# Graph layers on one core: the local numbers of the scores stage in bf16, its attribute transpose one step earlier

## The chip, the cores and the metric

The kernel runs on one core of one Trainium2 chip. The time is the device time of one execution in microseconds. Three runs of the kernel before gave 5438.61, 5443.80 and 5426.68 us, median 5438.61.

## What is computed

Four graph layers follow each other over 3125 nodes of 128 features and 100000 edges, each with a residual and a layer norm. The change lies in the second one, attention over edges. Cut to what matters:

```
q = (x @ Wq + bq).reshape(n, H, C)          # 4 heads of 32
k = (x @ Wk + bk).reshape(n, H, C)
v = (x @ Wv + bv).reshape(n, H, C)
e = (edge_attr @ We).reshape(-1, H, C)      # 32 attributes of each edge
kj = k[src] + e
vj = v[src] + e
alpha = jnp.einsum('ehc,ehc->eh', q[dst], kj) / np.sqrt(C)
```

A softmax of alpha over the edges of each destination node and a weighted sum of vj follow.

## The kernel before, in words

Edges are sorted by destination and cut into tiles of 128. A *pair* is a tile together with a block of 128 nodes to which some of its edges go; there are up to 806 pairs. For each edge of a pair the *local number* is its destination's number less the first node of the block: 0 to 127 means that the edge belongs to the block, anything else that it does not. `index_stage` (L443 on) makes these numbers on VectorE (L558), stores them in DRAM as `loc` (L482) and transposes them for later stages. For the stair "dst", which is the stored one, there are two outputs, `local` and `source`.

`scores` (L1535 on) takes four pairs a step, 202 steps in all, six steps a round (WAYS = 6), with six buffers q = 0 to 5 for most tiles. 33 rounds run in hardware loops on TensorE and VectorE; GpSimd, SyncE and ScalarE have all steps written out. In a step:

- SyncE loads the attribute rows of four pairs (L1600) after the transpose of the same buffer one round before, and the row of 512 local numbers into one partition, `locr` (L1603), after that buffer's spread.
- GpSimd gathers the keys and values of 128 sources, four times (L1592). It waits for `added`, which VectorE's L1644 signals when the buffer is free again.
- TensorE makes, in this order: the transpose of the attribute rows (L1691), eight records of node products (four float32 products of a one-hot tile with `q`, two passes each, L1695), the attribute product (L1699, two passes), and the *spread*, a product of a row of ones with `locr` that copies the 512 numbers to all 128 partitions of PSUM (L1682), for the step two further on.
- ScalarE copies the transposed attributes to SBUF (L1611) and issues the store of k+e and v+e (L1616).
- VectorE makes the one-hot tile by comparing the spread numbers with the partition's number (L1637, "heat"), adds the attribute product to keys and values (L1644), multiplies by q (L1648) and sums over a head (L1651).

`attr_t` and the PSUM tiles have two buffers, which is why most waits of TensorE name the step two before (`before_last`). VectorE's order in a round (L1655 on) is heat 0, heat 1, then heat 2, score 0, heat 3, score 1, heat 4, score 2, heat 5, score 3, score 4, score 5. `softmax_maxima` (L1717 on) reads `loc` back from DRAM and compares it with 0 and 128 (L1821, L1822).

## Time and profile before

| | |
|---|---|
| profiled execution, device time | 5436.53 us |
| its span | 5434.8 us |
| median of the three runs | 5438.61 us |
| mean granted TensorE clock over the span | 0.694 |
| busy: TensorE, VectorE, ScalarE, GpSimd | 3062.4, 2231.2, 614.3, 3413.0 us |
| scores stage | about 1074 to 2380 us |

Busy times are sums over stages that have different limits, so the share of the whole span says little about one stage. In rows of groups and of the timeline, a name such as `sc_kve<-sc_kv,ps` reads "written from". "Idle before" is the time for which that engine had nothing just before the instruction, and the name behind the arrow is what ended the idle time by the profile's reading of semaphores. Starts of TensorE's records are measured; their ends are modelled.

### The profile page before, as it was taken

Reading aid. Unit: us, or ns where it says so; the run is one execution under the profiler, and the core shown is the slowest. Engines: PE = TensorE matmul, PEld = TensorE weight load, DVE = VectorE, ACT = ScalarE, POOL = GpSimd, SP = SyncE. Lnnn points to the kernel's source line nnn. Section 1 sums busy time; section 2 is a strip of 40 time slices with the busy share of each in tenths; the row PEclk is TensorE's granted clock in tenths of the full one; section 3 lists DMA queues with packets and bytes.
Section 4 is the critical chain, followed back from the end, with each engine's and each line's share of the span. In section 5 each row is a group of like instructions: output and inputs, shape, how many; then the busy total and the mean of one; then the engine's idle time right before and its main releaser. Section 6 shows DMA issues by size and latency. Waiting matters only on the chain. (4 is left out here: it accounts for less than half of the span.)

```text
span 5434.8 us, 50013 instructions
## 1 busy us (share of the span) xinstructions
PE 3062.4 (56%) x13750; PEld 2237.6 (41%) x13751; DVE 2231.2 (41%) x2709; ACT 614.3 (11%) x1076; POOL 3413.0 (63%) x3213
## 2 busy tenths in 40 slices
PE   3899989567777777744918633343333333333333
PEld 1788879233333333324917422232222323232223
DVE  7999985445555454568901331111111111101112
ACT  0455540000000000004701000000000000000000
POOL 2888868466556555657770356666666666666664
PEclk7999999666666666657958766665665656555555
DMA  5566667144444444425825332222222111111111
GB/s 177 157 181 192 177 198 230 37 131 138 132 133 139 132 135 130 139 87 159 259 62 195 136 100 70 69 64 60 60 59 60 48 46 46 45 46 46 46 46 46
DMA packets 498663, 599.91 MB, mean 110 GB/s; under 512 B 190115, under 2 KB 367441, under 8 KB 496248
## 3 DMA queue, kind: packets, MB, share of 16 engines
q0 software_dynamic: 117856, 246.12, 16.5%
q1 hardware_dynamic: 337751, 229.77, 14.8%
q10 hardware_dynamic: 42944, 122.68, 6.0%
q8 instruction: 51, 0.84, 0.1%
q14 instruction: 61, 0.49, 0.0%
HBM read 406.69 MB, written 204.36 MB: 112 GB/s over the span
## 5 line engine op out<-in xcount | busy, mean ns | idle before, releaser
L720 POOL DMA_INDIRECT rec_by_src<-rec,pos x782 | 1123.3, 1436 | 524.6 <-issue 238.9
L1132 PE MATMUL ps<-g_got,g_hot 128*128 x3224 | 687.5, 367 | 1225.8 <-issue 797.4
L1132 PEld LDWEIGHTS ps<-g_got,g_hot 128*128 128x128 f32 x3224 | 605.7, 272 | 1320.2 <-issue 1318.9
L1592 POOL DMA_INDIRECT sc_kv<-kv,d_src x806 | 761.8, 945 | 533.9 <-DVE sc_kve L1644 260.2
L1032 POOL DMA_INDIRECT g_got<-y_forward,d_msg x782 | 739.3, 945 | 381.8 <-issue 230.1
L1032 POOL DMA_INDIRECT g_got<-y_back,s_msg x782 | 737.8, 943 | 381.2 <-issue 233.5
L805 PE MATMUL ps<-ln_low,ln_hot 128*125 128x256 f32 x2848 | 620.3, 381 | 20.3 <-DVE ln_low L782 16.1
L805 PEld LDWEIGHTS ps<-ln_low,ln_hot 128*125 128x125 f32 x2848 | 535.6, 188 | 104.8 <-issue 24.4
L1043 DVE TENSOR_TENSOR g_hot<-ps,src_loc 128x1024 f32<-128x1024 f32 x101 | 120.6, 1221 | 992.5 <-remote 450.4
L1699 PE MATMUL ps<-w_e,sc_attrT 128*128 128x512 f32 x404 | 320.0, 887 | 246.0 <-ACT sc_attrT L1611 216.3
L1051 DVE TENSOR_TENSOR g_y<-ps,ms_b 128x384 f32<-128x384 f32 x75 | 41.8, 558 | 808.8 <-remote 474.2
L1695 PE MATMUL ps<-q,sc_hotT 128*128 x1616 | 308.5, 352 | 108.0 <-DVE sc_hotT L1637 92.0
L1644 DVE TENSOR_TENSOR sc_kve<-sc_kv,ps 128x1024 f32<-128x1024 f32 x202 | 244.9, 1212 | 239.2 <-DMA win_rows<-rec_by_dst,win_tilei 163.3
L1695 PEld LDWEIGHTS ps<-q,sc_hotT 128*128 128x128 f32 x1616 | 283.2, 262 | 130.2 <-issue 130.2
L1682 PE MATMUL ps<-sc_locr,ones 1*128 1x512 f32 x404 | 312.8, 864 | 10.4 <-issue 10.4
L1637 DVE TENSOR_SCALAR sc_hotT<-ps,part 128x512 f32<-128x512 f32 x202 | 148.0, 747 | 379.5 <-PE ps L1682 196.3
L1145 PE MATMUL ps<-ms_w,ms_xT 128*128 128x384 f32 x150 | 105.9, 800 | 250.0 <-DVE g_y L1051 166.0
L777 DVE TENSOR_TENSOR ln_low<-col,win_lo 128x1024 f32<-128x1024 f32 x178 | 219.7, 1234 | 4.9 <-PE ps L805 2.6
L782 DVE TENSOR_TENSOR ln_low<-ln_low,win_w 128x1024 f32<-128x1024 f32 x178 | 216.1, 1214 | 0.0
L779 DVE TENSOR_TENSOR ln_hot<-col,win_key 128x1000 f32<-128x1000 f32 x178 | 213.8, 1201 | 0.0
L2030 ACT ACTIVATE n_root<-n_var 128x25 f32<-128x25 f32 x1 | 0.2, 225 | 1812.2 <-DVE n_var L2019 1812.2
L828 ACT ACTIVATE ln_out<-ps 125x1024 f32<-125x1024 f32 x160 | 163.7, 1023 | 311.3 <-PE ps L805 294.5
(323 smaller groups left out, 3283.7 us busy)
## 6 DMA issues: line engine op xcount, KB each, us to landing
linked<-ln_out SPq DMA_DIRECT2D x320, 224.0 KB
ve<-sc_kve ACTq DMA_DIRECT2D x202, 256.0 KB
wv_ve<-ve SPq DMA_DIRECT2D x101, 512.0 KB
l_links<-linked SPq DMA_DIRECT2D x25, 800.0 KB
l_links<-linked ACTq DMA_DIRECT2D x25, 800.0 KB
f_links<-linked SPq DMA_DIRECT2D x25, 800.0 KB
f_links<-linked ACTq DMA_DIRECT2D x25, 800.0 KB
attr_pairs<-ln_feats POOLq DMA_DIRECT2D x7, 2048.0 KB
```

The lines of the kernel that those rows point to most:

```text
L720: pool.indirect_dma_start(out=dram["rec_by_src"], out_offset=bass.IndirectOffsetOnAxis(ap=S["pos"][:, c:c + 1], axis=0), in_=S["rec"][:, c ...
L777: dve.tensor_tensor(low[:, q, :, 0:P], S["col"][:, :].unsqueeze(1).to_broadcast([P, GROUP, P]), S["win_lo"][:, cols].unsqueeze(2).to_broad ...
L779: dve.tensor_tensor(hot[:, q], S["col"][:, 0:KEYS].unsqueeze(1).to_broadcast([P, GROUP, KEYS]), S["win_key"][:, cols].unsqueeze(2).to_broa ...
L782: dve.tensor_tensor(low[:, q, :, P:2 * P], low[:, q, :, 0:P], S["win_w"][:, cols].unsqueeze(2).to_broadcast([P, GROUP, P]), ALU.mult).then ...
L805: last = pe.matmul(ps[0:KEYS, bass.ds(slots[j], 2 * P)], hot[:, q, j, :], low[:, q, j, :], start=False, stop=True, skip_group_check=True)
L1032: pool.indirect_dma_start(out=got[:, (c % SLOTS) * D:(c % SLOTS + 1) * D], out_offset=None, in_=table, in_offset=bass.IndirectOffsetOnAxis ...
L1132: last = pe.matmul(ps[:, bass.ds(columns[j], width)], hot[:, q, j, :], got[:, bass.ds(slots[j], width)], start=False, stop=True, skip_grou ...
L1592: pool.indirect_dma_start(out=kv[:, q, j, :], out_offset=None, in_=dram["kv"], in_offset=bass.IndirectOffsetOnAxis(ap=S["d_src"][:, c:c + ...
L1644: dve.tensor_tensor(kve[:, q].rearrange("p a (k d) -> p k a d", d=D), kv[:, q].rearrange("p k (a d) -> p k a d", a=2), feat(q).rearrange(" ...
L1682: pe.matmul(spread_loc(q), S["ones"][0:1, :], locr[0:1, q, :], start=True, stop=True).then_inc(spread[q], 1)
L1695: pe.matmul(qe(q)[:, j * D:(j + 1) * D], hot_t[:, q, j * P:(j + 1) * P], S["q"][:, bass.ds(cols[j], D)], start=True, stop=True)
L1699: pe.matmul(feat(q), attr_t[:, q % 2, :], S["w_e"][:, :], start=True, stop=True).then_inc(product[q], 1)
```

## The change

The numbers are kept as bf16: a new tile `short` in the index stage is copied from the float32 numbers, and the store takes it; the DRAM array `loc`, the tile `locr` and the tile `mx_loc` become bf16. In `scores` a bf16 row of ones replaces the float32 one, so the spread is a product of two bf16 operands. A wait on `saved` in the index stage is taken out. The transpose of the attribute rows moves out of `step` into `turn_row`, and is issued for the next step behind the attribute product of this one, in front of the spread.

```
+        self.short = m.sb(name + "_short", [P, self.cols], BF16) if stored else None
...
-                                 wide[:, n % 2, 0:s.cols].rearrange("p (b e) -> p b e", e=P)).then_inc(saved, 16)
+                                 s.short[:, :].rearrange("p (b e) -> p b e", e=P)).then_inc(saved, 16)
...
-                        if s.stored and n - 2 == sum(len(t.outputs) for t in stairs[:k]):
-                            dve.wait_ge(saved, 32)
...
                         link(dve.tensor_copy(s.nodes[:, :].rearrange("p (b e) -> p b e", e=P), f[:, :, :, node_field]))
+                        link(dve.tensor_copy(s.short[:, :], wide[:, n % 2, 0:s.cols]))
...
-        locr = m.sb("sc_locr", [1, WAYS, STEP * P])
+        locr = m.sb("sc_locr", [1, WAYS, STEP * P], BF16)
+        ones = m.sb("sc_ones", [1, P], BF16)
...
+            dve.memset(ones[:, :], 1.0).then_inc(cleared, 1)
             dve.memset(S["alpha"][:, :, :], 0.0).then_inc(cleared, 1)
-            dve.wait_ge(cleared, 1)
+            dve.wait_ge(cleared, 2)
...
-                pe.matmul(spread_loc(q), S["ones"][0:1, :], locr[0:1, q, :], start=True, stop=True).then_inc(spread[q], 1)
+                pe.matmul(spread_loc(q), ones[:, :], locr[0:1, q, :], start=True, stop=True).then_inc(spread[q], 1)
+
+            def turn_row(i, q):
+                pe.wait_ge(featured[q], (i + 1) * 16)
+                before_last(pe, kept, q, i)
+                pe.transpose(turn(q), attr[:, q, :], S["ident"][:, :]).then_inc(turned[q], 1)
...
-                pe.wait_ge(featured[q], (i + 1) * 16)
-                before_last(pe, kept, q, i)
-                pe.transpose(turn(q), attr[:, q, :], S["ident"][:, :]).then_inc(turned[q], 1)
...
+            pe.wait_ge(cleared, 1)
             for q in range(2):
                 spread_row(0, q)
+            turn_row(0, 0)
             with pe.Fori(0, WHOLE) as i:
                 for q in range(WAYS):
                     step(i, q)
-                    if q + 2 < WAYS:
-                        spread_row(i, q + 2)
-                    else:
-                        spread_row(i + 1, q + 2 - WAYS)
+                    turn_row(i + (q + 1) // WAYS, (q + 1) % WAYS)
+                    spread_row(i + (q + 2) // WAYS, (q + 2) % WAYS)
...
-        loc = m.sb("mx_loc", [P, L])
+        loc = m.sb("mx_loc", [P, L], BF16)
...
-        "linked": scratch("linked", [2, WINDOWS, KEYS, P]), "loc": scratch("loc", [PAIR_COLS, P]),
+        "linked": scratch("linked", [2, WINDOWS, KEYS, P]), "loc": scratch("loc", [PAIR_COLS, P], BF16),
```

## Rows read from the trace of the kernel before

**Rows 1.** A stretch, scores stage: length; PE, PEld, DVE, ACT, POOL busy (count); clock

```profile
1500.00:1750.00 250.00, 182.12 (x501) 86.58 (x500) 124.86 (x156) 10.53 (x38) 149.79 (x159) 0.65 0.47 135
```

**Rows 2.** Groups of the scores stage: count, busy us, mean ns, idle before, releasers

```profile
L1592 POOL DMA_INDIRECT sc_kv<-kv,d_src x806 | 761.8, 945 | 533.9 <-DVE sc_kve L1644 260.2 <-issue 249.9 <-DVEq L1632 23.9
L1699 PE MATMUL ps<-w_e,sc_attrT 128*128 128x512 f32 x404 | 320.0, 887 | 246.0 <-ACT sc_attrT L1611 216.3 <-issue 29.6
L1682 PE MATMUL ps<-sc_locr,ones 1*128 1x512 f32 x404 | 312.8, 864 | 10.4 <-issue 10.4
...
L1644 DVE TENSOR_TENSOR sc_kve<-sc_kv,ps 128x1024 f32<-128x1024 f32 x202 | 244.9, 1212 | 239.2 <-DMA win_rows<-rec_by_dst,win_tilei 163.3 <-DMA dst_rows<-rec_by_dst,pair_tiles 63.1 <-issue 7.8
...
L1611 ACT ACTIVATE sc_attrT<-ps 128x128 f32<-128x128 f32 x202 | 56.0, 277 | 1263.9 <-remote 548.8 <-PE ps L1691 427.4 <-issue 280.2
```

**Rows 3.** Waits of the scores stage: us in total, times, longest us

```profile
POOL sc_kv L1592 <- DVE sc_kve L1644: 260.2, 79, 7.9
...
DVE sc_hotT L1637 <- PE ps L1682: 196.3, 67, 5.4
```

**Rows 4.** Timeline of one round: start us, us, instruction, idle before and releaser

```profile
1972.73 2.07 PE L1695 MATMUL ps<-q,sc_hotT 128*128 x8 [1.42 <-DVE sc_hotT L1637]
...
1976.44 2.07 PE L1682 MATMUL ps<-sc_locr,ones 1*128 1x512 f32 x2
...
1978.55 0.75 DVE L1637 TENSOR_SCALAR sc_hotT<-ps,part 128x512 f32<-128x512 f32 x1 [5.29 <-PE ps L1682]
...
1983.33 0.75 DVE L1637 TENSOR_SCALAR sc_hotT<-ps,part 128x512 f32<-128x512 f32 x1 [1.35 <-PE ps L1682]
...
1986.68 0.74 DVE L1637 TENSOR_SCALAR sc_hotT<-ps,part 128x512 f32<-128x512 f32 x1
1986.90 1.15 PE L1695 MATMUL ps<-q,sc_hotT 128*128 x8 [0.28 <-DVE alpha_cols L1651]
...
1988.85 1.12 PE L1682 MATMUL ps<-sc_locr,ones 1*128 1x512 f32 x2
...
1993.25 0.75 DVE L1637 TENSOR_SCALAR sc_hotT<-ps,part 128x512 f32<-128x512 f32 x1 [3.14 <-remote]
...
1995.68 2.08 PE L1699 MATMUL ps<-w_e,sc_attrT 128*128 128x512 f32 x2 [4.29 <-ACT sc_attrT L1611]
...
1997.68 2.07 PE L1682 MATMUL ps<-sc_locr,ones 1*128 1x512 f32 x2
...
1999.68 0.47 PE L1691 MATMUL ps<-ident,sc_attr 128*128 128x128 f32 x1
...
1999.95 1.92 PE L1695 MATMUL ps<-q,sc_hotT 128*128 x8
2003.87 1.22 DVE L1644 TENSOR_TENSOR sc_kve<-sc_kv,ps 128x1024 f32<-128x1024 f32 x1 [7.19 <-DMA win_rows<-rec_by_dst,win_tilei]
```

**Rows 5.** The same round in three stretches, columns as in Rows 1

```profile
1966.00:1982.00 16.00, 13.75 (x28) 6.20 (x28) 9.68 (x12) 0.83 (x3) 8.39 (x9) 0.50 0.43 127
1982.00:1992.00 10.00, 9.10 (x38) 4.57 (x37) 6.42 (x8) 0.55 (x2) 7.56 (x9) 1.00 0.59 167
1992.00:2004.00 12.00, 6.19 (x13) 2.88 (x13) 3.39 (x5) 0.39 (x2) 6.74 (x8) 0.51 0.40 118
```

**Rows 6.** Timeline of TensorE in the block sort: bf16 products at low, full clock

```profile
48.45 0.63 PE L712 MATMUL ps<-sb_mask,sb_strict 128*128 128x512 bf16 x1
48.87 0.63 PE L713 MATMUL ps<-sb_digits,sb_chosen 96*128 96x512 bf16 x1
...
54.87 0.39 PE L712 MATMUL ps<-sb_mask,sb_strict 128*128 128x512 bf16 x1 [0.34 <-DVE sb_place L671]
```

**Rows 7.** Timeline of the index stage's end

```profile
134.06 0.96 DVE L569 COPY dst_nodes<-dst_rows 128x896 f32<-128x896 f32 x1
...
135.10 0.41 SPq L482 DMA_DIRECT2D loc<-ix_wide  x1
...
144.21 0.91 DVE L771 MEMSET ln_zero<- 128x1024 f32 x1 [8.13 <-PEq L433]
```

More of the change, by code:

```diff
@@ L1705, in _ @@
                     step(i, q)
-                    if q + 2 < WAYS:
-                        spread_row(i, q + 2)
-                    else:
-                        spread_row(i + 1, q + 2 - WAYS)
+                    turn_row(i + (q + 1) // WAYS, (q + 1) % WAYS)
+                    spread_row(i + (q + 2) // WAYS, (q + 2) % WAYS)
             for q in range(TAIL):
                 step(WHOLE, q)
+                if q + 1 < TAIL:
+                    turn_row(WHOLE, q + 1)
                 if q + 2 < TAIL:
```

## Prediction

> **What bounds the kernel now.** I read the page first: the only products that the change touches are L1682 (the spread of the local numbers) and L1691 (the attribute transpose), both in the scores stage, which runs from 1074 to 2380 us. The view by stretches shows that no engine is full there: in 250 us GpSimd works 150, TensorE 182 and VectorE 125, and the granted clock is 0.65 [rows 1]. So the stage is set by a chain, and one has to see which engine waits for which. The groups of the stage give the parts: 806 gathers of 0.945 us on GpSimd with 249.9/806 = 0.31 us of issue each, and on TensorE, for each of the 202 steps, two records of 864 ns for the spread and two of 887 for the attribute product, beside node products and a transpose [rows 2].
>
> The waits say who is late. GpSimd stands 260.2 us for DVE L1644, which frees the slot of six that a gather fills [rows 3]. It has then filled all six, so it is ahead, and the pair VectorE and TensorE sets the pace. Gathers repeat every 1.25 us, so a round of six steps (24 gathers) could take 30.0 us; 159 gathers in 250 us are 37.7 us a round [rows 1, 2]. VectorE itself waits 196.3 us (67 times, two a round) for the spread of L1682, and 163.3 + 63.1 us (33 times, one a round) at L1644, where the view names a DMA of an earlier stage that shares the semaphore [rows 2, 3].
>
> The timeline of one round shows three things [rows 4]. First, behind a round's last score and the two one-hot tiles after it, VectorE waits 5.29 us for one chain of TensorE: node products from 1972.73, then the attribute product, then the spread from 1976.44, whose end at 1978.51 lets VectorE start at 1978.55. One step later it waits 1.35 us for the end of the next spread, before 1983.33. Secondly, the two steps after that are VectorE's: its one-hot tiles start 3.35 us apart (1983.33, 1986.68), TensorE keeps up and even waits 0.28 us (1986.90). Thirdly there are holds. The spread at 1988.85 should end at 1989.97, but the one-hot tile that needs it starts at 1993.25; the attribute product at 1995.68 should end at 1997.76, but the score that needs it starts at 2003.87, with 7.19 us of idle before it, although its gathers were filled long before and TensorE shows nothing after 2001.87. The profile does not say what TensorE does in a hold; I only see that its products are reported late, once or twice a round. The clock goes with it: 0.50 up to 1982, 1.00 up to 1992, 0.51 in the holds [rows 5].
>
> **The spread as a bf16 product.** Float32 has two records a step (404 for 202 steps) [rows 2], a bf16 product has one [rows 6]. At half clock a spread takes 2.01 us from start to start (1997.68 to 1999.68) [rows 4]. The nearest rows of a bf16 product with 512 columns stand in the block sort: at low clock 0.42 us from start to start and 0.63 to its end, at full clock 0.39 to its end [rows 6]. TensorE thus saves 1.59 us a step at 1.2 GHz and, against the 1.12 of 1988.85, 0.73 at 2.4 GHz. But only what lies on the chain counts:
> (a) The wait of 5.29 us. The chain ends with 2.07 us of spread; afterwards the transpose of the next step stands in front of the spread, so it ends with 0.27 (1999.68 to 1999.95) to 0.47 us of transpose and 0.63 of bf16 product: 0.90 to 1.10. Saved 0.97 to 1.17; I take 1.1.
> (b) The wait of 1.35 us. Here the spread takes 1.12 as at 1988.85 (both run at full clock), transpose and bf16 product half of 0.47 and 0.39. Saved 0.5 by that; TensorE also comes to it 1.1 earlier, but VectorE moves forward by the same 1.1. The clock rises by time, so a little more of this step runs at 1.2 GHz: I take 0.3, with 0 and 1.1 as ends.
> (c) In the two steps that VectorE sets, nothing: the 3.35 us are its own work.
> (d) The holds. If they last a fixed time from the product that they hold, nothing; if they end a fixed time after TensorE has run out of work, the spread at 1997.68 lies ahead of that end and gives its 1.59. The trace shows 1.9 us from TensorE's last record to the release here, but does not settle it. I take 0.7 from 0 to 1.59.
> Sum 2.1 us a round (ends 0.97, and 1.17 + 1.1 + 1.59 + 0.73 for the other hold = 4.6). 202 steps are 33.7 rounds: 71 us, from 33 to 155.
>
> **The transpose made one step ahead.** In program order it moves from behind the spread and the next step's register loads to in front of both. Its copy on ScalarE takes 0.28 us [rows 2] and has the node products of 1.15 to 1.92 us [rows 4] as cover, as before, so nothing is saved outside the holds; without that cover each step would pay the 0.28. Its cost, the transpose in front of the spread, is in (a) and (b). Its waits for the attribute rows and for the copy of two steps before now stand in front of a spread: behind them queue the spread and the next step, and VectorE's one-hot tile waits for that. SyncE's queue asks for the attribute rows as soon as a transpose has run, six steps ahead of use, and for the numbers when the spread has; both loads are issued a whole round ahead, the first now one spread earlier, and no wait in the rows names them. In a hold the next attribute product waits for a copy whose transpose is held; the new order gives the transpose only a spread more of lead, too little for a hold of 6 us.
>
> **The index stage.** VectorE gets one more copy of 128x896, float32 to bf16, in front of the signal that lets SyncE store the numbers. The copy of the nodes, of the same size, takes 0.96 us; the store leaves at 135.10, directly behind, and the next stage starts at 144.21, 8.13 us after VectorE ran out of work; the stores are what is left by then [rows 7]. This cost is on the path: +1.0 us, 0.5 to 1.1. The store halves its bytes (0 to -1; I take 0). The wait taken out was reached by no output here: the stored stair has two outputs, and it would have needed a third. In the maxima stage two comparisons of VectorE read bf16 in place of float32, and the memset of 128 ones stands in front of the scores' clearing: I take 0 for both, within the same 0.5 us either way.
>
> Sum: 71 - 1 = 70 us. The profiled execution took 5436.5 us (span 5434.8), 2.1 below the median of the runs shown: 5366.5 in its terms, **5368 us** against the median.
>
> **A rule on the clock.** The granted clock of this round is 0.50 (1.2 GHz) while TensorE works behind the hold, rises to 1.00 (2.4 GHz) from 1982 to 1992 and is 0.51 again through the next holds, in which TensorE has no records for 4.29 and 2 us [rows 4, 5]. The Trainium skill, "TensorE: Matmul & The Clock Gate", Part 1, says that the throttled state is the default and that activity releases it; by that, the trace agrees, and a change that takes products out of TensorE may lose clock.
>
> **The rivals.**
> 1. GpSimd sets the pace. If holds shrink or go with the shorter queue in front of them, VectorE no longer holds up the ring and the 260.2 us vanish: 5176, or any part of the way (5180 to 5280). For it: the idle of 3.14 and 7.19 us in front of 1993.25 and 2003.87 is 10.3 us a round, and 37.7 - 30.0 = 7.7 suffice. Against: nothing in the trace ties them to the float32 spread. 0.20.
> 2. No gain. The holds give the time back (they end by a clock of their own, and TensorE only waits longer in them), or a product of one row in bf16 takes as long as in float32: 5425 to 5445. 0.15.
> 3. Slower: more holds. Both holds begin where TensorE has caught up with VectorE; the wait at 1986.90 is the sign of it. With a shorter step it catches up sooner. A further hold costs 7.2 us. It decides from 2.1/7.2 = 0.3 more holds a round, ten in all; with one in every second round it is +3.6 - 2.1 = 1.5 us a round, +51: 5489; with one in each 5610. 0.10.
> 4. Slower: the clock stays at 1.2 GHz. The three steps between 1982 and 1992 are then TensorE's: 1.92 + 2.00 + 0.27 + 0.42 = 4.6 us (node products, attribute product from 1995.68 to 1997.68, transpose, bf16 spread) in place of 3.35, +3.75 a round against 2.1 saved, +55: 5494. The rule of the Trainium skill cited above points this way. Against: at low clock TensorE would still be busy without a pause, as it was before the clock rose. 0.06.
> My forecast has the rest, 0.49, with its own range 5281 to 5404.
>
> **How the numbers follow.** A measurement of this kernel can tell about 0.3%, 16 us. Faster by more: the forecast, rival 1 and a little of rival 2, 0.71. Within it: 0.13. Slower: rivals 3 and 4, 0.16. For 8 in 10 I go down into rival 1 to 5205 and up over rival 2 to 5450; rivals 3 and 4 and the floor at 5176 stay outside.
>
> **What would show it.** L1682 should have 202 records with a mean near 0.5 us instead of 404. VectorE's two waits a round for L1682 should sum to some 150 us and not 196.3. GpSimd's 260.2 us for L1644 should fall by about what the stage gains, near 70. The stage's end moves from 2380 to about 2310, and nothing changes elsewhere but 1 us before 145. Wrong would be: the waits at L1644 (226 us, 33 times) halved or gone (rival 1), more than ten more of them (rival 3), the stage's clock under 0.58 (rival 4), or L1682 at half its time and the stage as long as before (rival 2).

## The result, and the profile after

The changed kernel took 5445.3 us (median of 20 runs) where the kernel before took 5430.4 (20 runs beside it): a ratio of 1.0022, 95% interval 1.0014 to 1.0031. One of the 20 ran at 5787 us with a lower clock; the ratio is that of the other 19, whose median is 5444.5. That is 0.2% slower, within what counts here as no difference, and 77 us above the forecast of 5368. The profiled execution took 5446.2 us with a span of 5444.5. The granted clock over the stage rose, TensorE's busy time shrank, and the stage got no shorter (1299.8 us from first to last addition of keys and values, 1292.9 before). The stretch of [rows 1] again, in the changed kernel:

```profile
1500.00:1750.00 250.00, 132.33 (x460) 74.19 (x460) 125.14 (x155) 10.80 (x39) 149.10 (x159) 0.69 0.47 134
```

TensorE has 132 us of work there where it had 182, and GpSimd still only 159 gathers. The groups of the scores stage (columns of [rows 2]) show which engine waits:

```profile
L1593 POOL DMA_INDIRECT sc_kv<-kv,d_src x806 | 761.9, 945 | 547.0 <-DVE sc_kve L1646 279.5 <-issue 242.3 <-DVEq L1634 25.2
L1646 DVE TENSOR_TENSOR sc_kve<-sc_kv,ps 128x1024 f32<-128x1024 f32 x202 | 244.9, 1213 | 242.7 <-DMA win_rows<-rec_by_dst,win_tilei 114.4 <-DMA dst_rows<-rec_by_dst,pair_tiles 111.9 <-issue 12.7
L1639 DVE TENSOR_SCALAR sc_hotT<-ps,part 128x512 f32<-128x512 f32 x202 | 148.0, 747 | 380.6 <-remote 116.5 <-issue 92.5 <-PE ps L1684 89.9
L1684 PE MATMUL ps<-sc_locr,sc_ones 1*128 1x512 bf16 x202 | 95.3, 473 | 10.6 <-DVEq L1634 10.6
```

The spread (L1684) is 202 records of 473 ns (the prediction said near 0.5 us), 95.3 us in place of 312.8. The line to read is the third. The one-hot tiles of VectorE (L1639) stand idle for 380.6 us in front, against 379.5 before, where the group of L1637 was split into 196.3 us for the spread, 105.7 "remote" and 43.9 "issue". The waits say how that sum is now split:

```profile
POOL sc_kv L1593 <- DVE sc_kve L1646: 279.5, 74, 8.2
DVE sc_hotT L1639 <- remote: 116.5, 23, 19.9
DVE sc_hotT L1639 <- issue: 92.5, 34, 11.6
DVE sc_hotT L1639 <- PE ps L1684: 89.9, 28, 4.7
DVE sc_hotT L1639 <- DMA l_links<-linked: 81.6, 16, 10.3
```

The spread is named for 89.9 us (28 times) where it was 196.3 us (67 times) [rows 3]; the other names (remote, issue, and a DMA of an earlier stage that shares the semaphore) sum to 290.7 us and were 183.2. A name alone does not part the two causes, because an idle time with a late report in it also holds the time until the product's own end. So I split each idle time of VectorE at the modelled end of the product that it waits for. What lies ahead of that end is the chain: VectorE would wait for it in any case. What lies behind it is a late report. The trace has the times of the reports themselves for most products: of the late parts of over 1 us, 334 of 344 us before and 411 of 446 us in the changed kernel end within 0.3 us of such a report, and for the rest none is on record. The gathers are no rival for the waits of the addition: the last gather that such an addition reads was issued more than 4 us, mostly some 30 us, before it.

| us of VectorE's idle time | chain, one-hot tiles | late reports, one-hot tiles | chain, additions | late reports, additions |
|---|---|---|---|---|
| before | 233.1 | 146.4 | 37.2 | 202.0 |
| changed kernel | 147.6 | 233.0 | 15.7 | 227.0 |

The chain got shorter by 85.5 + 21.5 = 107 us, and the late reports grew by 86.6 + 25.0 = 112 us. What the change gave, late reports of TensorE took again. One of them in the timeline:

```profile
2026.74 0.27 PE L1689 MATMUL ps<-ident,sc_attr 128*128 128x128 f32 x1
2026.95 0.39 PE L1684 MATMUL ps<-sc_locr,sc_ones 1*128 1x512 bf16 x1
...
2028.89 1.15 PE L1699 MATMUL ps<-q,sc_hotT 128*128 x8 [1.55 <-issue]
...
2035.30 0.28 ACT L1612 ACTIVATE sc_attrT<-ps 128x128 f32<-128x128 f32 x1 [10.34 <-remote]
2035.33 0.75 DVE L1639 TENSOR_SCALAR sc_hotT<-ps,part 128x512 f32<-128x512 f32 x1 [6.58 <-DMA l_links<-linked]
2035.62 2.08 PE L1703 MATMUL ps<-w_e,sc_attrT 128*128 128x512 f32 x2 [5.58 <-ACT sc_attrT L1612]
```

The transpose should end at 2027.01 and the spread at 2027.34. ScalarE, which waits for the one, starts at 2035.30, and VectorE, which waits for the other, at 2035.33: two products with ends 0.33 us apart are reported together, 8 us late. This is the hold of the prediction, and longer: the two in [rows 4] had lasted some 3 and 6 us. By the recorded starts the products of the next step begin at 2028.89, in the middle of it, so TensorE goes on working while its reports are held.

### The profile page after: what moved, and what is told of

It is laid out like the page before. It is cut to its first block and busy times, and to the rows that moved or that the text cites. A ratio compares the mean times of both kernels' runs of the same rounds, so it can differ in the third digit from the quotient of the medians.

```text
span 5444.5 us, 49642 instructions
## 1 busy us (share of the span) xinstructions
PE 2806.7 (52%) x13546; PEld 2169.7 (40%) x13549; DVE 2229.9 (41%) x2711; ACT 614.5 (11%) x1076; POOL 3413.9 (63%) x3213
## 5 line engine op out<-in xcount | busy, mean ns | idle before, releaser
L1132 PE MATMUL ps<-g_got,g_hot 128*128 x3224 | 689.2, 365 | 1214.9 <-issue 858.1
L1132 PEld LDWEIGHTS ps<-g_got,g_hot 128*128 128x128 f32 x3224 | 604.6, 270 | 1310.2 <-issue 1309.2
L805 PE MATMUL ps<-ln_low,ln_hot 128*125 128x256 f32 x2848 | 619.4, 380 | 19.5 <-DVE ln_low L782 15.6
L805 PEld LDWEIGHTS ps<-ln_low,ln_hot 128*125 128x125 f32 x2848 | 534.8, 188 | 103.9 <-issue 23.8
L1699 PEld LDWEIGHTS ps<-q,sc_hotT 128*128 128x128 f32 x1616 | 263.5, 248 | 433.2 <-issue 433.2
L1703 PE MATMUL ps<-w_e,sc_attrT 128*128 128x512 f32 x404 | 303.0, 843 | 250.5 <-ACT sc_attrT L1612 227.0
L1646 DVE TENSOR_TENSOR sc_kve<-sc_kv,ps 128x1024 f32<-128x1024 f32 x202 | 244.9, 1213 | 242.7 <-DMA win_rows<-rec_by_dst,win_tilei 114.4
L1639 DVE TENSOR_SCALAR sc_hotT<-ps,part 128x512 f32<-128x512 f32 x202 | 148.0, 747 | 380.6 <-remote 116.5
L1612 ACT ACTIVATE sc_attrT<-ps 128x128 f32<-128x128 f32 x202 | 56.0, 277 | 1269.2 <-remote 688.6
```

The lines of the kernel that those rows point to most:

```text
L805: last = pe.matmul(ps[0:KEYS, bass.ds(slots[j], 2 * P)], hot[:, q, j, :], low[:, q, j, :], start=False, stop=True, skip_group_check=True)
L1132: last = pe.matmul(ps[:, bass.ds(columns[j], width)], hot[:, q, j, :], got[:, bass.ds(slots[j], width)], start=False, stop=True, skip_grou ...
L1646: dve.tensor_tensor(kve[:, q].rearrange("p a (k d) -> p k a d", d=D), kv[:, q].rearrange("p k (a d) -> p k a d", a=2), feat(q).rearrange(" ...
L1699: pe.matmul(qe(q)[:, j * D:(j + 1) * D], hot_t[:, q, j * P:(j + 1) * P], S["q"][:, bass.ds(cols[j], D)], start=True, stop=True)
L1703: pe.matmul(feat(q), attr_t[:, q % 2, :], S["w_e"][:, :], start=True, stop=True).then_inc(product[q], 1)
```

## Experiments

All times are medians beside runs of the kernel before on the same chip; the ratio is against those. The runs were made in four groups, and each group had its own chip and time (the first and the fourth had the same chip; that of the first result is not on record). I number the groups, because that turned out to matter. "Idle of VectorE" is the sum of the idle time in front of its one-hot tiles and of its addition of keys and values, read from the groups of the stage as above, chain and late reports together: 379.5 + 239.2 = 618.7 us before, 380.6 + 242.7 = 623.3 after.

**Group 1: the parts apart.** First only the bf16 spread, the transpose back in its own step:

```diff
             def step(i, q):
+                turn_row(i, q)
...
-                    turn_row(i + (q + 1) // WAYS, (q + 1) % WAYS)
```

> The change without the transpose moved: it stands again at the head of its own step; numbers and row of ones stay bf16. Theory A (holds come when TensorE has caught up with VectorE and waits for it; a shorter step brings more of them): as many holds as with the whole change, some 45 long ones, and a time of 5440 to 5455. Theory B (the moved transpose is what costs, because it stands in front of the spread): faster than before, near 5370.

5393.7 us, ratio 0.9939 (0.9923 to 0.9956). Neither theory: the one part alone is worth 33 us by the ratio (25 by the medians), where both together had lost beside the first result's kernel before. Idle of VectorE 586.7 us. Then only the transpose ahead, with the numbers and the spread in float32:

```diff
-        locr = m.sb("sc_locr", [1, WAYS, STEP * P], BF16)
+        locr = m.sb("sc_locr", [1, WAYS, STEP * P])
```

> The change with everything in float32 and only the transpose moved. Theory A: the step is as long as before the change, so about 34 long holds, one a round, and 5425 to 5445. Theory B: the transpose of 0.27 to 0.47 us now lengthens the two waits a round for the spread, so 5445 to 5460.

5430.9 us, 1.0008 (0.9986 to 1.0030): nothing, inside Theory A's range, with 621.1 us of idle. The spread is named for 144.0 us where it was 196.3, but by the split at the modelled end the chain in front of the one-hot tiles is longer, 247.4 us against 233.1 before (235.4 in the other profile of that kernel): the transpose stands in it. In front of the additions it is shorter, 14.8 against 37.2. Late reports are 358.9 us in all, against 348.4. Then both parts, TensorE's loop over the rounds written out:

```diff
-            with pe.Fori(0, WHOLE) as i:
+            for i in range(WHOLE):
```

> The changed kernel with TensorE's hardware loop over the rounds of the scores written out in full; the same instructions otherwise, and waits against constants in place of registers. If the holds belong to the loop (a branch back, code that is loaded, registers), they go and the stage is set by GpSimd, near 5190. If they belong to how TensorE waits for VectorE (theory A), they stay and the time is 5435 to 5455.

5390.0 us, 0.9939 (0.9922 to 0.9955), in neither range (5435 to 5455, or near 5190); idle 566.7 us. The late reports stay (50 gaps of over 2 us in front of one-hot tiles, the stage's first two left out, where the changed kernel has 69 and the kernel before 64; 413.9 us of late reports in all), so neither the loop's branch nor its code is their cause. Last, eight more short bf16 products behind each spread, in case a product is reported only when others push it out:

```diff
+            def push(q):
+                at = (4 + q % 2) * BANK + 2 * P
+                for _ in range(8):
+                    pe.matmul(ps[:, at:at + 64], ones[:, :], ones[:, 0:64], start=True, stop=True)
...
                     spread_row(i + (q + 2) // WAYS, (q + 2) % WAYS)
+                    push(q)
```

> The changed kernel with eight bf16 products of one row and 64 columns behind each spread, into a part of PSUM that nobody reads; they are extra work and change no result. Theory A in its sharper form (what TensorE has finished is reported late when nothing follows it while TensorE waits for VectorE): the small products follow the attribute product, transpose and spread at once, so most holds go: 5190 to 5300. If the holds have nothing to do with what follows: 5440 to 5470, as the eight cost some 0.3 us a step on TensorE, which waits for VectorE anyway.

5459.2 us, 1.0069 (1.0052 to 1.0085), inside the second range. Reports are late with eight products right behind them as well, so that theory falls. The groups of this kernel:

```profile
L1646 DVE TENSOR_TENSOR sc_kve<-sc_kv,ps 128x1024 f32<-128x1024 f32 x202 | 244.9, 1212 | 112.4 <-DMA win_rows<-rec_by_dst,win_tilei 42.3 <-DMA dst_rows<-rec_by_dst,pair_tiles 36.9 <-issue 29.5
L1639 DVE TENSOR_SCALAR sc_hotT<-ps,part 128x512 f32<-128x512 f32 x202 | 148.0, 747 | 527.9 <-remote 228.0 <-DMA l_links<-linked 191.1 <-issue 62.6
```

The waits changed place: 112.4 us in front of the addition, 527.9 in front of the one-hot tiles, 640.3 in all. By the split, 210.5 us of that is chain, where the three profiles of the changed kernel have 159 to 163, and 429.8 late reports, where they have 424 to 460: the loss of this run lies in the chain, which the small products lengthen.

**Group 2: the same questions on another chip.** Spread ahead of the transpose; the bf16 spread alone with the loop written out; the block numbers' register loads left out; three of four gathers left out.

```diff
-                    turn_row(i + (q + 1) // WAYS, (q + 1) % WAYS)
                     spread_row(i + (q + 2) // WAYS, (q + 2) % WAYS)
+                    turn_row(i + (q + 1) // WAYS, (q + 1) % WAYS)
```

> The changed kernel with one thing swapped: behind the products of a step TensorE now does the spread of two steps ahead first and the attribute transpose of the next step behind it, still ahead of the next node products. Measured so far: bf16 spread alone 0.9939, transpose ahead alone 1.0008, both 1.0022. Theory A (what the turn costs beside a bf16 spread is its place in front of the spread on VectorE's chain, its wait for the attribute rows included): the loss goes, 0.993 to 0.997 of the kernel before, and the late reports come back to the 56 gaps of over 2 us in front of the one-hot tiles that bf16 alone had. Theory B (the transpose ahead makes the reports of TensorE late wherever it stands, since it brings the two short instructions together at the end of a step): still 1.000 to 1.003, with 66 to 71 such gaps.

4657.0 us, 0.9995 (0.9985 to 1.0004), in neither range.

```diff
             def step(i, q):
+                turn_row(i, q)
...
-            with pe.Fori(0, WHOLE) as i:
+            for i in range(WHOLE):
```

> The bf16 spread alone (the transpose in its own step, as before the change), and TensorE's loop of the scores written out in place of the register loop. Measured: bf16 alone 0.9939 with the loop, both parts of the change 1.0022 with the loop and 0.9939 without it. Theory A (the loop and the transpose ahead each add a cost of their own): 0.985 to 0.989, the sum of the two gains. Theory B (the gains are one and the same, some phase that both disturb): 0.992 to 0.996, as each alone. Late reports should be 52 to 56 gaps before the one-hot tiles in either.

4657.6 us, 0.9991 (0.9982 to 1.0001), in neither range.

```diff
-                _, cols = nc.values_load_multi_w_load_instructions(
...
-                              S["q"][:, bass.ds(cols[j], D)], start=True, stop=True)
+                              S["q"][:, j * D:(j + 1) * D], start=True, stop=True)
```

> The changed kernel with the register loads of the block numbers left out: the node products all read the first four blocks of the query table, so the scores are not those of the reference. Everything else of TensorE's sequence is unchanged. Theory A (the late reports hang on the loads of the registers that stand between two steps in TensorE's queue: the sequencer waits for them and what it has finished is told late): the long waits for TensorE, 71 gaps of over 2 us before the one-hot tiles and 23 before the keys' addition, fall to under half, and the time to 0.96 to 0.98 of the kernel before. Theory B (they have nothing to do with the loads): 60 to 75 gaps stay and the time is within 0.99 to 1.005, the loads' own issue time being the only gain.

4658.1 us, 0.9993 (0.9983 to 1.0003). This kernel leaves out the choice of the query block and the next one leaves out gathers, so neither computes the reference's scores. The time is Theory B's, but the 60 to 75 gaps that it wants are not there, so the run does not tell the two apart: what the loads do in a hold stays untried.

```diff
-                for j in range(size(n)):
+                for j in range(size(n) if i == 0 else 1):
```

> The changed kernel with three of the four gathers of each step left out from the second round on: their slots keep old rows, so the scores are wrong. GpSimd then works a quarter of its 762 us and the gathers' transfers are a quarter. Theory A (the pair of TensorE and VectorE with its late reports sets the pace, and those do not come from the gathers): the late reports stay at one in 4 to 5 steps, the stage stays near its 1300 us, within 60 us of the changed kernel's, and GpSimd waits nearly the whole stage. Theory B (late reports come from the gathers' traffic or descriptor writing): they go, and the stage falls to what TensorE and VectorE need, 202 steps of 3.4 to 4.4 us, 700 to 900 us, 0.91 to 0.93 of the kernel before.

4453.4 us, 0.9556 (0.9538 to 0.9574). The stage falls into Theory B's 700 to 900 us, but not because the gathers went: the other three kernels of the group, with all their gathers, have no late report either.

The surprise is in the line that none of the expectations had: on this chip the kernel before took 4660.8 us (25 runs, 4652 to 4668), 14% less than on the others. The same program, the same data. The kernel before and the changed kernel have no profile from this chip; the groups of the stage in the first of these kernels (both parts of the change, spread first) are:

```profile
L1593 POOL DMA_INDIRECT sc_kv<-kv,d_src x806 | 762.0, 945 | 253.6 <-issue 245.2 <-DVEq L1634 8.4
L1646 DVE TENSOR_TENSOR sc_kve<-sc_kv,ps 128x1024 f32<-128x1024 f32 x202 | 245.6, 1216 | 196.6 <-DMA sc_kv<-kv,d_src 195.6 <-PE ps L1703 0.9
L1639 DVE TENSOR_SCALAR sc_hotT<-ps,part 128x512 f32<-128x512 f32 x202 | 147.5, 745 | 131.8 <-PE ps L1684 131.8
```

GpSimd waits for nothing but its own issue (245.2 us over 806 gathers, 0.30 each): it sets the pace, 806 x 1.25 = 1008 us for a stage that takes 1005, not 1293. VectorE waits for the gathers' data and for the spread, each named rightly, and no report is late by more than 4 us: none of the 629 on record in the stage, where of 435 in the changed kernel of the first result 143 are 4 to 16 us late. By the split VectorE has 1.5 us of late reports in front of the one-hot tiles. This is rival 1 of the prediction, brought about by the chip or the time of the runs and not by the change, and there both variants that compute the same as the change, spread first and spread alone, lie within 0.1% of the one before. The changed kernel itself did not run there. With three of four gathers gone the stage is 806 us (from its first addition to its last), 4.0 us a step, which is what VectorE and TensorE need by themselves when nothing is held.

The other stages tell what the holds are. In the message stage, which the change does not touch, the kernel before had TensorE's records like this in its first profile (weight loads and products of L1132; at 4459.90 sixteen loads had taken 3.49 us):

```profile
4459.90 3.49 PEld L1132 LDWEIGHTS ps<-g_got,g_hot 128*128 128x128 f32 x16 [6.57 <-issue]
...
4473.42 0.29 PEld L1132 LDWEIGHTS ps<-g_got,g_hot 128*128 128x128 f32 x1 [2.33 <-issue]
4474.81 0.37 PE L1132 MATMUL ps<-g_got,g_hot 128*128 x1 [2.43 <-issue]
4476.21 0.29 PEld L1132 LDWEIGHTS ps<-g_got,g_hot 128*128 128x128 f32 x1 [2.50 <-issue]
4477.61 0.37 PE L1132 MATMUL ps<-g_got,g_hot 128*128 x1 [2.43 <-issue]
```

From 4472 to 4493 a record comes every 1.40 us, loads and products in turn, so a pair takes 2.80 us where 3.49/16 = 0.22 is usual, and nothing is named that TensorE would wait for. I call this a slow episode. As runs of at least four records that each start 0.65 to 3 us after the last, the trace has 41 of them between 3150 and 5400 us, 796 us in all; a looser count, which an expectation below uses, has 37 with 841. The same records show the late reports too:

```profile
4495.82 0.59 PE L1132 MATMUL ps<-g_got,g_hot 128*128 x2 [0.83 <-issue]
...
4495.94 3.49 DVE L1043 TENSOR_TENSOR g_hot<-ps,src_loc 128x1024 f32<-128x1024 f32 x3 [37.97 <-remote]
```

VectorE's one-hot tiles of this stage wait for groups of sixteen products. The groups that TensorE ended at 4453.52 and 4463.67 by the model are reported at 4495.81 and 4495.97, 42 and 32 us late, when the episode is over. Of the 41 episodes 37 have such a report, over 4 us late, inside them or within 6 us of their end, for products that had ended by the model before the episode was 3 us old. So holds and episodes stand in the same records, and not only on the same chips. On the chip of group 2 there is none, and the same stretch of that stage stands so, first before, then spread first:

```profile
3500.00:4500.00 1000.00, 366.24 (x1571) 281.28 (x1572) 139.98 (x150) 2.42 (x6) 646.29 (x685) 0.61 0.20 56
```

```profile
3500.00:4500.00 1000.00, 379.63 (x1645) 348.90 (x1643) 127.63 (x110) 0.00 (x0) 746.10 (x792) 0.59 0.20 53
```

685 gathers in 1000 us against 792, at a granted clock of 0.61 and 0.59: the clock does not show the difference. The longest single hold stands between the two stages, in front of the product of L1407, and in the kernel before it is 86.4 us of TensorE's idle time:

```profile
2757.18 0.37 PE L1402 MATMUL ps<-ident,skip 128*128 128x128 f32 x1 [1.62 <-issue]
2843.97 2.07 PE L1407 MATMUL ps<-f_aggT,w_l 128*128 128x512 f32 x2 [86.42 <-issue]
```

The product of L1402 that it hangs on is reported 85.7 us late. This idle time is 55.8 to 88.5 us in all fourteen profiles outside group 2, and 2.0 to 2.3 us in the four of group 2. Between the kernel before of group 3 and the spread-first kernel, the spans differ by 786 us: 38 ahead of the first gather of the scores, 266 in the gathers of the scores, 208 from there to the first gather of the messages, 275 behind it.

The index sort, where TensorE works without a pause, has no episodes to speak of on either chip (one of 2 us in the changed kernel): its products (L805) are 2848 of 380 ns, 619.4 us in the changed kernel and 618.4 in the spread-first kernel.

```profile
L805 PE MATMUL ps<-ln_low,ln_hot 128*125 128x256 f32 x2848 | 619.4, 380 | 19.5 <-DVE ln_low L782 15.6
```

```profile
L805 PE MATMUL ps<-ln_low,ln_hot 128*125 128x256 f32 x2848 | 618.4, 380 | 17.9 <-DVE ln_low L782 14.4
```

**Group 3: both kernels again, with holds and episodes.** This chip has both (38 episodes in the message stage of the changed kernel, 35 before).

> The kernel before, unchanged, with a profile on whatever chip these four runs get. What has come out so far: on the chip of the first result it took 5430 us, on the chip of the bf16, transpose, written-out and pushed runs 5419, on the chip of the last four runs 4661. In the 5430 us profile TensorE's records of the message stage stand 1.40 us apart, weight load to product, in 37 episodes that fill 841 of 2250 us; in the 4661 us profiles there is none. Theory A (the long waits for TensorE in the scores stage are the same episodes, and a chip has them or has not): either 5400 to 5450 us with some 37 episodes and some 66 waits of over 2 us before the one-hot tiles, or 4650 to 4670 us with no episode and nearly none of those waits. Theory B (two things): one of them without the other.

5419.1 us, 0.9990 (0.9974 to 1.0005) of the other runs of itself: the old time, 35 episodes, 70 waits of over 2 us in front of the one-hot tiles. This is Theory A. By now it can be said of all profiles of this study: the fourteen with holds in the scores stage (group 4 is in the count) have 35 to 50 episodes in the message stage, the four of group 2 have neither.

> The changed kernel, unchanged, beside the kernel before on the same chip. Theory A (the change is worth nothing where GpSimd's gathers set the pace of the scores stage, and is swallowed by TensorE's slow episodes where they are): on a chip without episodes 0.9985 to 1.0005 of the kernel before, on one with them 1.000 to 1.004. Theory B (the loss of 0.2% is the transposes' own cost, whatever the chip): 1.001 to 1.004 on either.

5394.3 us, **0.9945** (0.9928 to 0.9962). The kernel that had been 0.2% slower is 0.55% faster here. This misses both theories.

> The bf16 spread alone, the transpose in its own step, beside both kernels on this chip. Theory A (its gain of 0.6% came from fewer or shorter slow episodes of TensorE on that chip): on a chip without episodes 0.9985 to 1.0005; on one with them 0.990 to 0.998. Theory B (it is the shorter chain to VectorE's one-hot tiles, whatever the chip): 0.992 to 0.996 on either.

5400.9 us, 0.9942 (0.9920 to 0.9963), as in group 1, and the same as the changed kernel beside it: here the transpose ahead costs nothing. With the 0.9991 of the same spread in group 2, there with the loop written out, this is Theory A: the gain is made where holds are.

The two lines of VectorE for the kernel before and for the changed one, both of this group, show where the 25 us come from:

```profile
L1644 DVE TENSOR_TENSOR sc_kve<-sc_kv,ps 128x1024 f32<-128x1024 f32 x202 | 244.8, 1212 | 211.9 <-DMA win_rows<-rec_by_dst,win_tilei 135.8 <-DMA dst_rows<-rec_by_dst,pair_tiles 55.9 <-PE ps L1699 12.1
L1637 DVE TENSOR_SCALAR sc_hotT<-ps,part 128x512 f32<-128x512 f32 x202 | 148.1, 747 | 404.8 <-PE ps L1682 185.7 <-remote 123.9 <-issue 69.3
```

```profile
L1646 DVE TENSOR_TENSOR sc_kve<-sc_kv,ps 128x1024 f32<-128x1024 f32 x202 | 245.0, 1213 | 268.0 <-DMA win_rows<-rec_by_dst,win_tilei 189.9 <-DMA dst_rows<-rec_by_dst,pair_tiles 61.8 <-PE ps L1703 9.5
L1639 DVE TENSOR_SCALAR sc_hotT<-ps,part 128x512 f32<-128x512 f32 x202 | 147.8, 746 | 315.1 <-remote 85.0 <-PE ps L1684 83.2 <-issue 79.8
```

By the split at the modelled end the chain falls from 235.4 to 142.5 us in front of the one-hot tiles and from 39.1 to 16.1 in front of the additions, 116 us together, about as in the first result. Late reports grow from 169.4 to 172.6 and from 172.8 to 251.9, 82 us together: they took back most of it, not all. 33.6 us are left, and the stage is 32 us shorter (1258.7 against 1291.1, first addition to last).

The fourth run leaves out three of the four node products of a step:

```diff
-                for j in range(STEP):
+                for j in range(1):
                     pe.matmul(qe(q)[:, j * D:(j + 1) * D], hot_t[:, q, j * P:(j + 1) * P],
```

> The changed kernel with three of the four node products of each step left out in the scores stage (12 of its 16 float32 weight loads and products), so the scores are wrong; every wait and every transfer stays. Theory A (TensorE's slow episodes come with the work it does): on a chip with episodes the waits of over 2 us before the one-hot tiles fall from 71 to under 30, and the scores stage loses over 100 us of its 1300, 0.96 to 0.98 of the kernel before. Theory B (they come by a clock of their own): 55 to 75 such waits and 0.985 to 1.0. On a chip without episodes the gathers set the pace in either theory, and it is 0.997 to 1.0.

5354.4 us, 0.9869 (0.9852 to 0.9885), 0.74% below the changed kernel of the group.

```profile
L1646 DVE TENSOR_TENSOR sc_kve<-sc_kv,ps 128x1024 f32<-128x1024 f32 x202 | 244.8, 1212 | 66.8 <-DMA dst_rows<-rec_by_dst,pair_tiles 39.8 <-issue 10.2 <-DMA win_rows<-rec_by_dst,win_tilei 7.2
L1639 DVE TENSOR_SCALAR sc_hotT<-ps,part 128x512 f32<-128x512 f32 x202 | 150.7, 747 | 480.2 <-DMA l_links<-linked 423.1 <-issue 48.1 <-PE ps L1684 6.6
```

Half of TensorE's products in the stage are gone (1200 records where the changed kernel of the group has 2406), but they are busy for 659 us where those were for 667, because the granted clock fell. The same stretch, changed kernel first, then this one (columns as in [rows 1]):

```profile
1500.00:1750.00 250.00, 129.36 (x479) 72.95 (x477) 126.92 (x159) 10.82 (x39) 152.19 (x161) 0.71 0.48 137
```

```profile
1500.00:1750.00 250.00, 136.29 (x250) 52.54 (x249) 135.45 (x168) 11.36 (x41) 157.87 (x167) 0.50 0.50 142
```

Of the 583 us of idle only 36 are gone. The chain is nearly off the path (32 us by the split, 159 in the changed kernel), and late reports grew from 424 to 515 us: of 126 us that the chain gave, they took 90. There are 61 waits of over 2 us in front of the one-hot tiles and the ratio is 0.9869; both lie in Theory B's ranges (55 to 75, and 0.985 to 1.0), not in Theory A's (under 30, and 0.96 to 0.98). Since the clock changed with the work, the run does not show what fewer products at the old clock would do.

**Group 4: where the episodes fall.** The chip of group 1 again, at another time.

> The changed kernel, unchanged, once more on whatever chip these four get. It came out at 1.0022 of the kernel before on the first chip and at 0.9945 on another; both have the slow episodes of TensorE, and its scores stage took 1299.8 and 1258.7 us in the two profiles. Theory A (the gain is real where episodes are, and the 1.0022 is one chip's): with episodes 0.992 to 0.997 here; without them, at 4660 us, 0.9985 to 1.0005. Theory B (with episodes the sign is open, since their number in the stage is what is left of the change): anything from 0.990 to 1.004.

5434.0 us, **1.0006** (0.9994 to 1.0018). Theory B, whose range of 0.990 to 1.004 was wide enough for nearly anything: with holds the sign is open. Its idle time splits as in the first result: 159.0 us of chain, 453.4 of late reports (the spread is named for 77.5 us).

```diff
+            for k in range(3):
+                dve.memset(S["alpha"][:, :, :], 0.0).then_inc(delayed, 1)
+                dve.wait_ge(delayed, k + 1)
             dve.memset(ones[:, :], 1.0).then_inc(cleared, 1)
```

> The changed kernel with the scores stage begun some 10 us later: three more memsets of the score columns, 3.04 us each in the trace, one behind the other, ahead of the stage's first wait. Nothing within the stage differs. Theory A (the time within the stage is the same wherever its start falls against the episodes): 9 to 11 us, 0.2%, above the changed kernel of this call. Theory B (it depends on how episodes and rounds fall together): it differs by more than 15 us from that, in either direction. Without episodes it is 9 to 11 us more in either theory.

5451.5 us, 1.0040 (1.0026 to 1.0053), 17.5 us above the changed kernel. Its first gather starts 6.7 us later (1083.6 against 1076.9). The stage was to begin 9 to 11 us later and begins 6.7 later, and the rest, some 10 us, is about as large as the uncertainty of the two ratios together; inconclusive.

> The changed kernel with the spread of two steps ahead done in front of the transpose of the next step. It stood at 0.9995 on the chip without episodes. Theory A (the transpose costs VectorE's chain 0.27 to 0.47 us where it stands in front of the spread): on a chip with episodes 0.1 to 0.3% below the changed kernel of this call. Theory B (its place is hidden): within 0.1% of it. Without episodes all lie within 0.1%.

5420.7 us, 0.9978 (0.9967 to 0.9990): 13 us less than the changed kernel with the transpose first, and the intervals do not meet. That is Theory A's sign and size (0.1 to 0.3%).

```profile
L1646 DVE TENSOR_TENSOR sc_kve<-sc_kv,ps 128x1024 f32<-128x1024 f32 x202 | 244.9, 1212 | 231.9 <-DMA win_rows<-rec_by_dst,win_tilei 149.1 <-DMA dst_rows<-rec_by_dst,pair_tiles 64.4 <-issue 16.0
L1639 DVE TENSOR_SCALAR sc_hotT<-ps,part 128x512 f32<-128x512 f32 x202 | 147.9, 746 | 375.4 <-DMA l_links<-linked 134.2 <-remote 119.2 <-PE ps L1684 82.0
```

Yet the chain is not what got shorter: it is 167.4 us here against 159.0, and late reports are 439.9 against 453.4. That the transpose's place is the cause rests on the time alone.

> The bf16 spread with the transpose in its own step and TensorE's loop of the scores written out: the version with most of the single gains in it. Theory A (the gains of the single parts add up where episodes are): 0.985 to 0.990 of the kernel before. Theory B (each only removes TensorE time that the episodes then take, so the gain has a ceiling): 0.992 to 0.996. Without episodes 0.9985 to 1.0005.

5421.9 us, 0.9982 (0.9973 to 0.9992), in neither range. The single gains do not add up; in group 4 all of them together are worth 0.2%.

## Why the prediction was wrong

**The prices held.** Two of the prediction's sizes can be read off one round of the changed kernel:

```profile
1989.22 0.60 PE L1684 MATMUL ps<-sc_locr,sc_ones 1*128 1x512 bf16 x1
...
1989.86 0.75 DVE L1639 TENSOR_SCALAR sc_hotT<-ps,part 128x512 f32<-128x512 f32 x1 [4.04 <-issue]
...
1994.02 0.75 DVE L1639 TENSOR_SCALAR sc_hotT<-ps,part 128x512 f32<-128x512 f32 x1 [0.73 <-DMA l_links<-linked]
```

(a) The chain's wait is 4.04 us; 5.29 - 1.1 = 4.19 had been forecast. The bf16 product takes 0.60 and 0.39 us; [rows 6] has 0.63 and 0.39. (b) The second wait is 0.73 where 1.05 was forecast, but it is no chain any more: the spread for it started at 1992.06 and ended at 1992.45, and VectorE asked for it at 1993.29, so the 0.73 is a late report and the chain's 1.35 us are gone whole. Over the stage, the two waits for the spread were to fall from 196.3 us to some 150. They are named for 89.9, 83.2 and 77.5 us in three profiles, and by the split the chain in front of the one-hot tiles fell by 85 and 93 us and that in front of the additions by 22 and 23. So the sum of (a) and (b), 1.4 us a round or 47 us, was too small for the chain, not too large.

**The step that failed is (d), and with it the sum over 33.7 rounds.** It took the holds as a fixed part of each round: they would last as long as before or give up to 1.59 us, with 0 as the worst end. The end below zero was missing. The holds took back 112 us of the chain's 107 in the first profile and 82 of 116 in group 3. The prediction says itself that the profile does not tell what TensorE does in a hold, and then multiplies a gain by the rounds as if the holds stood still. Holds do not come at a fixed place of a round: in the trace of before they came about once a round, 25 to 41 us apart; in the changed kernel they come mostly every 25 to 33 us (reports at 1978.97, 2009.76, 2035.24, 2060.78, 2094.39), and last longer. Counted from the modelled end of a product to its report (reports within 2 us of one another are one hold, of which the longest counts), the stage of before has 36 holds of over 6 us, 338 us in all, and that of the changed kernel 43 with 449 us; in group 3 it is 37 with 293 us and 44 with 469. These counts move by several with the rule of counting, and about a quarter of the stage's products have no report on record; the order of before and after does not change.

The measured 5445 lies inside the wide range of 5205 to 5450, at its upper edge, but not by the forecast's own path, whose range ended at 5404: it was rival 2, given 0.15, that reached there.

**The rivals.** Rival 3 had the right direction for the holds (more hold in the changed kernel; that TensorE's catching up brings them on is not shown) and near enough the point of balance, ten more holds of 7.2 us: there were seven more in each of the two pairs of profiles, each on average some 1 to 3 us longer. Its time, 5489, assumed half a hold a round more. Its sign was to be more waits at L1644; they fell, from 33 to 25, and most of the growth stood in front of the one-hot tiles. Rival 2 (no gain, because holds "end by a clock of their own") names the same give-back and gave 5425 to 5445, and its sign, L1682 at half its time or less and the stage as long as before, is what came: it is the part of the prediction that was right. Rival 1 set out that the stage falls to the gathers' pace once holds go; group 2, without them, shows that floor (1005 us), but no change of TensorE's work reached it: with 12 of its weight loads and products gone from each step, 547 us of idle were left. Rival 4 did not happen in the changed kernel: the granted clock of the stretch rose from 0.65 to 0.69.

**The clock rule.** The prediction cited the Trainium skill, "TensorE: Matmul & The Clock Gate", Part 1, for the risk that less work costs clock. The runs have it both ways. With the shorter spread TensorE was busy for 50 us less in 250, and the granted clock rose (0.65 to 0.69). With half of the products left out it fell from 0.71 to 0.50, the low level for the whole stretch; that is the rule's direction, and what rival 4 feared. The rows also show that the granted clock is no sign of holds: 0.61 in the message stage with episodes, 0.59 without.

**The transpose.** It was forecast to gain nothing by itself, and was 1.0008 alone. Its place in front of the spread was charged with 0.27 to 0.47 us in (a) and about half of 0.47 in (b): 0.5 to 0.7 us a round, 17 to 24 us. With the transpose ahead alone the chain in front of the one-hot tiles grew by 14 us, which is near the charge. Putting it behind the bf16 spread gained 13 us in group 4, but there the profiles show no shorter chain, and in group 3 the changed kernel and the bf16 spread alone are equal (0.9945 and 0.9942). So what its place costs beside a bf16 spread is not shown.

**The index stage.** The added copy takes 0.63 us, not 0.96, and the store of the numbers leaves 0.70 us later:

```profile
135.09 0.63 DVE L569 CAST dst_short<-ix_wide 128x896 bf16<-128x896 f32 x1
...
135.80 0.41 SPq L483 DMA_DIRECT2D loc<-dst_short  x1
```

The next stage's first memset starts at 144.21 and 145.17 in the two profiles of the kernel before and at 144.28 and 144.07 in those of the changed kernel beside them, so the forecast's 1 us is not to be seen. Between the last gather of the scores and the first of the messages lie 803.1 and 797.6 us before and 792.6, 793.2 and 800.1 after: nothing of the change shows there.

**What stays open.** What a chip does in an episode, and why one of four groups had none, no profile says. Group 2 differs from the others in chip and in time, so which of the two decides is not shown; and every time on record comes with a span and a granted clock that the profiler took, so it is not excluded that profiling has a part in the holds. That holds and episodes are one thing rests on their coming and going together in eighteen profiles and on the late reports inside the episodes. And why the same change came out at 1.0022, 0.9945 and 1.0006 where there are holds is only bounded: the chain gave 107 and 116 us in the two groups with both profiles, and the holds took all of it and seven tenths. Whether chip, time or the phase of the rounds decides the rest, the shifted run did not settle.

## To carry to other kernels

When a profile shows waits whose named releaser had long been done, split each wait at that releaser's end, and find out whether other stages, which the change does not touch, show the same engine slow for no reason. A gain on that engine must then be priced with "the stall takes it back" as one end of its range: here the stalls stayed when the loop was written out and when half of the products were gone. Run the kernel before on more than one chip before forecasting a few tenths of a per cent: here it ran 14% faster on another chip, which turned the bound from TensorE to the gathers.

## What the runs showed of the hardware

- In fourteen of eighteen profiles TensorE falls into slow episodes in the message stage: a weight load and product every 2.80 us in place of 0.22, for up to 44 us at a time, some 800 of 2250 us in the kernel before, with a granted clock of 0.61; the one read of the four without episodes has 0.59. The index sort, with TensorE busy for 619 us, had none over 2 us.
- In the same fourteen, TensorE's completions are reported late: in the scores stage up to 16 us after the modelled end as a rule and up to three at once, in the message stage 32 and 42 us where an episode was read, in front of L1407 85.7 us. The waiting engines' idle time is then put down to other names.
- The whole kernel is 5420 to 5440 us with episodes and 4661 without.
- With half of the products of a stage left out, the granted clock fell from 0.71 to 0.50, and the products that were left (group 3) were busy for as long (659 us) as all had been (667).
- A bf16 product of one row by 512 columns takes 0.60 us to its end at 1.2 GHz and 0.39 at 2.4, where float32 needs two records, 2.07 and 1.12 us.
